# Moving the norm guard, the layer-norm shift and the cell marks from VectorE to GpSimd in an audio tower kernel

## The chip, the cores and the metric

The kernel runs on one core of a Trainium2 chip. The metric is device time in microseconds (us) for one execution of the whole program. Engines are named as the profile names them: PE (TensorE), DVE (VectorE), ACT (ScalarE), POOL (GpSimd), SP (SyncE).

## What is computed

The reference takes `x` of 16 x 375 x 64 and works in three stages.

1. A convolution of nine taps to 128 features, scaled by the norm of its window, through tanh, a bias and ReLU. This gives `h0`, 16 batches of 367 positions.
2. A layer norm of `h0`, attention with one head and three windows that share their scores, an output projection, a residual and a second layer norm; added to `h0`.
3. A third layer norm `hn`, then a product-key feed-forward layer. Cut to what matters here:

```
q  = layernorm(hn @ Wq.T + bq) * ln_g + ln_b        # 8 heads of 64
q0, q1 = halves of 32;   s0, s1 = l2norm(q0) @ l2norm(keys0).T, the same for 1
sc0, ix0 = top_k(s0, 16);  sc1, ix1 = top_k(s1, 16)
fs, pos  = top_k(all sums sc0 + sc1, 16);  fi = the sums of the indices there
w = softmax(fs);   out = sum over heads of (gelu(hn . down[fi]) * w) @ up[fi]
```

`l2norm(x)` is `x / max(norm, 1e-12)`; that maximum is the guard of the norms.

## The kernel before, in words

A batch has 367 positions and is worked in three overlapping tiles of 124 (t = 0, 1, 2). `lnr` and `lnm` (reciprocal deviation and shift) exist for three layer norms i = 0, 1, 2: of `h0`, of `res` (after attention) and of `h` (before the feed-forward layer).

Each engine runs one `body(c)` per batch: a list of steps written out by hand, in which steps of different batches and tiles are interleaved (`c + 1` is the next batch). The first and last bodies are unrolled, the middle ones run in a loop of two. Nothing reorders the work: an engine goes through its list, and a step waits on semaphores for what it needs. POOL issues no DMA. SP loads `x` and stores `o_sb`.

What the change and the prediction touch, by engine:

- **Norm guard and scale.** ACT squares the query and leaves the sums `nss` (`q_norms`, L793). POOL's `q_std` forms `qvar`, `std` (a power, L541) and `qguard` (L542). DVE's `q_guard` (L1303) takes `nmx = max(nss, qguard)`, 16 columns. POOL's `q_scale` (L549) raises it to the power -0.5.
- **Layer norms.** DVE's `p1_stats` (L1249, `bns`) and `p1_moments` (L1259, `bna`) make mean and variance; POOL's `p1_rstd` adds epsilon (L509, `lnv`) and takes the power (L510, `lnr`); DVE's `p1_shift` (L1266) makes `lnm = -mean * lnr`; ACT's `p1_ln` (L706) applies both.
- **Choosing cells.** POOL's `rank_sums` scales the ranked values (L569) and forms 50 candidate sums per head, `cs`, in two halves, and the sums of indices `ce` (L575 to L581). DVE's `choose` (L1391, L1393) runs four steps: the 8 best, their removal into `cr`, the next 8, their removal. DVE's `mark` (L1401) writes `taken`: 4096 where `cr` holds the fill value, else 0, 124 x 400. DVE's `sum_exps` and `invert_sums` (L1412, `wrec`) form the softmax denominator. POOL's `select` multiplies `taken` with `ce` (L591) and with the exponentials (L593), `normalise` finishes the weights (L600, L603) with a copy by ACT between (L823).
- **After that.** PE turns and merges the weights (L1088, L1099), ACT writes the digits `eh` (L841), DVE compares them (`one_high`, L1339, `oh`; `one_low`, L1346 and L1349) and forms `wl` (`low_weights`, L1358), PE multiplies `oh` and `wl` (`scatter`, L1114), DVE forms `prod` (L1367), PE the output, DVE `o_sb`.
- **Attention, around it.** PE's `p1_ax` (L1023), `p1_wo` (L1030), DVE's `p1_res` (L1294), PE's scores (L1000), DVE's `p1_smax` (L1279), POOL's `sbias` (L516), ACT's `probs` (L729), DVE's `rden` (L1287).
- **Head of the next batch.** POOL's `p1_norm` (L491, L492, `wnorm`), DVE's `p1_tscale` (L1235), POOL's `p1_h0` (L499, L501, `h0`), then `p1_stats` for i = 0.

POOL's list between two of these points matters below:

```
rank_sums(c,1,0)  p1_rstd(c+1,2)  rank_sums(c,1,1)  p1_norm(c+2)  q_scale(c,2)
p1_h0(c+2)  q_std(c+1,0)  p1_rstd(c+2,0)  rank_sums(c,1,2)  select(c,1)  normalise(c,1)
rank_sums(c,2,0)  rank_sums(c,2,1)  q_scale(c+1,0)
```

(the last line is the top of the next body, in the same names). DVE's list from `choose(0,3)` goes on with `low_weights(2)`, `mark(0)`, `sum_exps(0)`, `q_guard(1)`, `invert_sums(0)`, ranking, `product(2)`, ranking, `p1_res`.

Of the kernel before, what the change touches and what calls it, by code (L numbers as in the profile page):

```python
# [66 lines left out]
def build(nc, x, tok_kernel, tok_bias, wq, bq, wk, bk, wo, bo, gamma, beta, fwq, fbq, lng, lnb,  # L67
# [5 lines left out]
    with ctx:  # L73
        def sb(name, shape, dt=f32):
            return ctx.enter_context(nc.sbuf_tensor(name, shape, dt))

        def sem(name):
            return ctx.enter_context(nc.semaphore(name))
# [348 lines left out]
        def _(pool):  # L427
# [75 lines left out]
            def p1_rstd(c, i):  # L503
                b = c.b
                link = linker(pool, ln_rstd[i], 2, b)
                pool.wait_ge(ln_stats[i], 2 * (b + 1))
                wait(pool, ln_shift[i], b)
                wait(pool, (xl_ready, xh_ready, hn_ready)[i], b)
                link(g.tensor_tensor(lnv[i][:, :], bna[i][:, :, 1], eps3[:, :], ALU.add))  # L509
                link(g.tensor_tensor(lnr[i][:, :], lnv[i][:, :], power[0:NT, 0, 0:3], ALU.pow), wait=False)  # L510

# [21 lines left out]
            def q_std(c, t):  # L533

                n = c.tile(t)
                link = linker(pool, std_ready, 3, n)
                pool.wait_ge(qss_ready, n + 1)
                wait(pool, std_turned, n)
                wait(pool, nmx_ready, n)
                link(g.tensor_tensor(qvar[:, :], qss[:, :], eps8[:, :], ALU.add))  # L540
                link(g.tensor_tensor(std9[:, 0:H], qvar[:, :], power[0:NT, 1, 0:H], ALU.pow), wait=False)  # L541
                link(g.tensor_tensor(qguard[:, :], qvar[:, :], guard8[:, :], ALU.mult), wait=False)  # L542

            def q_scale(c, t):

                n = c.tile(t)
                pool.wait_ge(nmx_ready, n + 1)
                wait(pool, vals_scaled, 2 * (n - 1))
                g.tensor_tensor(qscale[c.slot(t)][:, :, :].rearrange("p h s -> p (h s)"), nmx[:, :, :].rearrange("p h s -> p (h s)"),  # L549
                                power[0:NT, 0, :], ALU.pow).then_inc(qscale_ready, 1)  # L550

            def rank_sums(c, t, part):
# [5 lines left out]
                if part == 0:  # L558
                    pool.wait_ge(ranked, 16 * n + 6)
                    wait(pool, chosen, 11 * n - 7)  # L560
# [24 lines left out]
            def select(c, t):  # L585

                n = c.tile(t)
                pool.wait_ge(cells_ready, 3 * (n + 1))
                pool.wait_ge(chosen, 11 * n + 9)
                wait(pool, cells_turned, n)  # L590
                g.tensor_tensor(wcell[:, 2, :, :], taken[:, :, :], ce[:, :, :], ALU.mult).then_inc(weights, 1)  # L591
                pool.wait_ge(exp_ready, n + 1)
                g.tensor_tensor(wsel[:, :, :], taken[:, :, :], cx[:, :, :], ALU.mult).then_inc(weights, 1)  # L593

            def normalise(c, t):

                n = c.tile(t)
                pool.wait_ge(weights, 4 * n + 2)
                pool.wait_ge(chosen, 11 * (n + 1))
# [45 lines left out]
        def _(act):  # L645
# [534 lines left out]
        def _(dve):  # L1180
# [81 lines left out]
            def p1_shift(c, i):  # L1262
                b = c.b
                dve.wait_ge(ln_rstd[i], 2 * (b + 1))
                wait(dve, (xl_ready, xh_ready, hn_ready)[i], b)
                v.scalar_tensor_tensor(out=lnm[i][:, :], in0=bna[i][:, :, 0], scalar=-1.0, in1=lnr[i][:, :],  # L1266
                                       op0=ALU.mult, op1=ALU.mult).then_inc(ln_shift[i], 1)

# [20 lines left out]
            def p1_res(c):  # L1289
# [5 lines left out]
                                xb[:, :, :].rearrange("p t d -> p (t d)"), ALU.add).then_inc(res_ready, 1)  # L1295

            def q_guard(c, t):

                n = c.tile(t)
                dve.wait_ge(nss_ready, n + 1)  # L1300
                dve.wait_ge(std_ready, 3 * (n + 1))
                wait(dve, qscale_ready, n)
                v.tensor_tensor(nmx[:, :, :], nss[:, :, :], qguard[:, :].unsqueeze(2).to_broadcast([NT, H, 2]), ALU.max).then_inc(nmx_ready, 1)  # L1303

# [90 lines left out]

            def mark(c, t):

                n = c.tile(t)
                wait(dve, weights, 4 * n)
                dve.wait_ge(chosen, 11 * n + 8)  # L1400
                v.tensor_scalar(taken[:, :, :], cr[:, :, :], NEG / 2, WSCALE, ALU.is_lt, ALU.mult).then_inc(chosen, 1)  # L1401

            def sum_exps(c, t):
# [4 lines left out]
            def invert_sums(c, t):  # L1408
                n = c.tile(t)
                wait(dve, weights, 4 * n)  # L1410
                dve.wait_ge(chosen, 11 * n + 10)
                v.reciprocal(wrec[:, :], wsum[:, :]).then_inc(chosen, 1)  # L1412


            def body(c):
                do(choose, c + -1, 0, 3)
                do(low_weights, c + -2, 2)
                do(mark, c + -1, 0)
                do(sum_exps, c + -1, 0)
                do(q_guard, c + -1, 1)  # L1420
                do(invert_sums, c + -1, 0)
# [30 lines left out]
                do(p1_moments, c + 1, 0)  # L1452
                do(mark, c + -1, 1)
# [3 lines left out]
                do(p1_shift, c + 1, 0)  # L1457
                do(rank, c + -1, 2, 0, 1)
# [66 lines left out]
```

## Time and profile before

| | |
|---|---|
| time, median of 3 runs | 1542.49 us (1540.91 to 1542.98) |
| the profiled execution: time, span | 1543.36 us, 1541.5 us |
| granted TensorE clock over the span | 0.719 |
| busy: PE, DVE, ACT, POOL | 1254.0, 1324.0, 899.9, 962.9 us |
| HBM traffic | 5 GB/s over the span |

A busy share is an average over the whole span. What a step is worth is read from the chain of waits: at each point the engine that ends the wait counts, whether or not it is the busiest. In a timeline row the number in brackets is the time for which the engine sat idle before the row, and what ended it. Rows of one engine that follow each other overlap a little.

### The profile page before, as it was taken

The numbers are of one execution on the slowest core, as the hardware profiler recorded it, in microseconds if no ns is written. First come the engines' busy times: TensorE is split into PE (matmuls) and PEld (weight loads), VectorE is DVE, ScalarE is ACT, GpSimd is POOL, SyncE is SP. The second block draws the span as 40 slices with busy tenths as digits, with TensorE's granted clock in tenths as the row PEclk, the third lists the DMA queues.
The fourth block names the chain that finished last, engine by engine and source line by source line (L and its number), as shares of the span: only waits on it lengthen the run. The fifth ranks groups of instructions, "written<-read, shape, count | busy, mean of one in ns | idle before, by whom it ended". The sixth has DMA issues, their size and how long they took to land.

```text
span 1541.5 us, 41273 instructions
## 1 busy us (share of the span) xinstructions
PE 1254.0 (81%) x9637; PEld 731.0 (47%) x9637; DVE 1324.0 (86%) x10216; ACT 899.9 (58%) x4107; POOL 962.9 (62%) x1870
## 2 busy tenths in 40 slices
PE   2558989798888888898888878898888889888873
PEld 1324445454546454554645554464545455463343
DVE  3116999999999989898899999899798999999895
ACT  1345675766575674656567476656656666655532
POOL 4233867576766857576575757577485767656452
PEclk9667687787767777685777688576676868675555
DMA  1000000000000000000000000000000000000000
GB/s 38 13 1 6 2 5 8 4 10 4 10 4 3 9 5 9 4 10 3 5 10 4 9 5 10 4 8 6 4 9 4 5 4 6 3 4 4 4 3 7
DMA packets 21499, 10.17 MB, mean 7 GB/s; under 512 B 13495, under 2 KB 21099, under 8 KB 21228
## 3 DMA queue, kind: packets, MB, share of 16 engines
q1 hardware_dynamic: 21228, 7.27, 1.9%
q8 instruction: 83, 1.36, 0.4%
q14 instruction: 188, 1.54, 0.3%
HBM read 4.25 MB, written 3.01 MB: 5 GB/s over the span
## 4 chain that ended last, share of the span: by engine, by line
DVE 47%; PE 21%; POOL 10%; ACT 10%; issue 10%; SPq 1%; DVEq 1%; ACTq 0%; POOLq 0%; DMA 0%
DVE idx L1326 14%; DVE val L1324 8%; DVE scores L1329 7%; PE bankM L1114 4%; DVE cr L1393 3%; DVE oh L1339 3%; PE bankQ L1054 3%; POOL cs L575 2%; DVE best L1391 2%; PE bankS L1078 2%; POOL std L541 2%; PE bankS L1077 2%; ACT act_g L770 1%; ACT sq_junk L779 1%; DVE wl L1358 1%
## 5 line engine op out<-in xcount | busy, mean ns | idle before, releaser
L1326 DVE FIND_INDEX8 idx<-val,scores 124x8 uint16<-124x64 f32 x1536 | 304.3, 216 | 0.0
L1324 DVE MAX8 val<-scores 124x8 f32<-124x64 f32 x1536 | 210.8, 207 | 15.8 <-ACT scores L800 15.1
L1114 PE MATMUL bankM<-wl,oh 128*128 128x16 f16 x5952 | 163.0, 172 | 46.2 <-DVE wl L1358 46.2
L1114 PEld LDWEIGHTS bankM<-wl,oh 128*128 128x128 f16 x5952 | 160.0, 101 | 63.2 <-issue 39.9
L793 ACT ACTIVATE ns_junk<-bankQ 124x32 f32<-124x32 f32 x768 | 139.2, 278 | 36.0 <-PE bankQ L1067 36.0
L1339 DVE TENSOR_SCALAR oh<-eh 128x992 f16<-128x992 int16 x384 | 136.4, 424 | 25.3 <-ACT eh L841 25.3
L1329 DVE MATCH_REPLACE8 scores<-val,scores 124x64 f32<-124x64 f32 x768 | 151.3, 206 | 0.0
L549 POOL TENSOR_TENSOR qscale<-nmx,power 124x16 f32<-124x16 f32 x48 | 139.6, 2908 | 10.2 <-DVE nmx L1303 10.1
L793 ACT ACTIVATION_READ_ACCUMULATOR ns_junk<-bankQ 124x1 f32 x768 | 139.5, 291 | 0.0
L1077 PE MATMUL bankS<-wgk,hnT 128*124 128x512 f32 x192 | 121.0, 716 | 0.0
L1078 PE MATMUL bankS<-bias9k,std9T 9*124 9x512 f32 x192 | 120.8, 711 | 0.0
L1011 PE MATMUL banks<-diag,probs 124*124 124x124 f32 x672 | 107.6, 326 | 12.7 <-ACT diag L738 12.5
L575 POOL TENSOR_TENSOR cs<-val_s 124x64 f32<-124x64 f32 (+4 forms) x480 | 109.2, 261 | 7.5
L591 POOL TENSOR_TENSOR wcell<-taken,ce 124x400 f16<-124x400 f32 x48 | 56.8, 1184 | 87.4 <-DVE taken L1401 46.1
L1011 PEld LDWEIGHTS banks<-diag,probs 124*124 124x124 f32 x672 | 100.1, 236 | 19.7 <-ACT diag L738 18.7
L1326 DVE MATCH_VALUE_LOAD idx<-val,scores 124x8 f32 x1536 | 108.3, 70 | 0.0
L1122 PE MATMUL bankM<-up_x,prod 128*124 128x128 f32 x384 | 91.6, 418 | 18.9 <-DVE prod L1367 18.9
L516 POOL TENSOR_TENSOR sbias<-smax,minus_scale 124x3 f32<-124x3 f32 x48 | 14.4, 301 | 148.1 <-DVE smax L1279 148.1
L779 ACT ACTIVATE sq_junk<-bankQ 124x64 f32<-124x64 f32 x384 | 79.3, 234 | 43.6 <-PE bankQ L1055 43.5
L823 ACT ACTIVATE wcell<-wn 124x400 f16<-124x400 f32 x48 | 27.6, 576 | 127.6 <-POOL wn L600 127.6
L1045 PE MATMUL bankQ<-hnT,down_x 128*128 128x372 f32 x128 | 80.8, 725 | 20.5 <-ACT ns_junk L793 11.2
L1122 PEld LDWEIGHTS bankM<-up_x,prod 128*124 128x124 f32 x384 | 83.8, 319 | 25.4 <-DVE prod L1367 23.8
(195 smaller groups left out, 3302.6 us busy)
## 6 DMA issues: line engine op xcount, KB each, us to landing
x_in<-in_x SPq DMA_DIRECT2D x16, 93.8 KB
x_in<-in_x SPq DMA_DIRECT2D x16, 62.5 KB
out<-o_sb SPq DMA_DIRECT2D x16, 62.0 KB
out<-o_sb SPq DMA_DIRECT2D x16, 61.0 KB
out<-o_sb SPq DMA_DIRECT2D x16, 60.5 KB
x_in<-in_x SPq DMA_DIRECT2D x16, 31.0 KB
fwq_in<-in_L_ffn_Wq SPq DMA_DIRECT2D x1, 256.0 KB
conv_w<-in_L_tok_kernel SPq DMA_DIRECT2D x2, 128.0 KB
```

The source lines that it names most:

```text
L549: g.tensor_tensor(qscale[c.slot(t)][:, :, :].rearrange("p h s -> p (h s)"), nmx[:, :, :].rearrange("p h s -> p (h s)"), power[0:NT, 0, :], ...
L575: g.tensor_tensor(dst[:, :, at:at + m], src[:, :, 0, a:a + 1].to_broadcast([NT, k, m]), src[:, :, 1, 0:m], ALU.add)
L793: last = a.activation(ns_junk[:, i, :], bankQ[0:NT, i * HALF:(i + 1) * HALF], ACT.Square, accum_out=nss[:, i // 2, i % 2:i % 2 + 1])
L1011: last = e.matmul(bankB[0:NT, k * NT:(k + 1) * NT], probs[t][w][:, OFF[k]:OFF[k] + NT], diag[:, w, :], start=w == windows[0], stop=w == wi ...
L1077: e.matmul(part, hnT[c.par][:, t, :], wgk[:, 2 * k:2 * k + 2, :].rearrange("p k n -> p (k n)"), start=True, stop=False)
L1078: last = e.matmul(part, std9T[:, :], bias9k[:, 2 * k:2 * k + 2, :].rearrange("p k n -> p (k n)"), start=False, stop=True)
L1114: last = e.matmul(coef[:, g, :, :], oh[:, k, g, :, :].rearrange("p v t -> p (v t)"), wl[:, part, k, :, TG * g:TG * (g + 1)], start=k + par ...
L1122: last = e.matmul(ffn, prod[:, l, :], up_x[:, l, :], start=l == 0, stop=l == EL - 1)
L1324: last = v.max(out=v_[:, hd, s, best8], in_=src[:, hd, s, :])
L1326: last = v.max_index(out=i_[:, hd, s, best8], in_max=v_[:, hd, s, best8], in_values=src[:, hd, s, :])
L1329: last = v.match_replace(out=src[:, hd, s, :], in_to_replace=v_[:, hd, s, best8], in_values=src[:, hd, s, :], imm_value=NEG)
L1339: last = v.tensor_scalar(by_shift[:, :, :, value, :], eh[:, :, :, :].rearrange("p s k (g t) -> p s (k g) t", t=TG), float(value), None, AL ...
```

## The change

Three steps leave DVE's list. `q_guard` becomes three operations in POOL's `q_scale`: subtract `qguard`, maximum with 0, add `qguard` (then the power, as before). `p1_shift` becomes a multiplication of the mean by -1 and a product at the end, in POOL's `p1_rstd`. `mark` becomes the first operation of POOL's `select`. The order of all other steps stays, on all engines. The semaphore `chosen` counts ten per tile instead of eleven, and a new semaphore `marked` lets DVE's `choose` of the next tile overwrite `cr` only once it was read.

```diff
 def p1_rstd(c, i):                                  # POOL
-    link = linker(pool, ln_rstd[i], 2, b)
+    link = linker(pool, ln_rstd[i], 3, b)
     pool.wait_ge(ln_stats[i], 2 * (b + 1))
-    wait(pool, ln_shift[i], b)
     wait(pool, (xl_ready, xh_ready, hn_ready)[i], b)
-    link(g.tensor_tensor(lnv, bna[.., 1], eps3, ALU.add))
-    link(g.tensor_tensor(lnr, lnv, power, ALU.pow), wait=False)
+    link(g.tensor_tensor(lnv, bna[.., 1], eps3, ALU.add), wait=False)
+    link(g.tensor_scalar(lnn, bna[.., 0], -1.0, None, ALU.mult))
+    link(g.tensor_tensor(lnr, lnv, power, ALU.pow))
+    g.tensor_tensor(lnm, lnn, lnr, ALU.mult).then_inc(ln_shift[i], 1)
 def q_std(c, t):                                    # POOL
-    wait(pool, nmx_ready, n)
 def q_scale(c, t):                                  # POOL
-    pool.wait_ge(nmx_ready, n + 1)
+    pool.wait_ge(nss_ready, n + 1)
+    spread = qguard[:, :].unsqueeze(2).to_broadcast([NT, H, 2])
+    pool.wait_ge(std_ready, 3 * (n + 1))
+    g.tensor_tensor(nmx, nss, spread, ALU.subtract).then_inc(nmx_ready, 1)
+    pool.wait_ge(nmx_ready, 3 * n + 1)
+    settled(pool, passed_pool)
+    g.tensor_scalar(nmx, nmx, 0.0, None, ALU.max).then_inc(nmx_ready, 1)
+    pool.wait_ge(nmx_ready, 3 * n + 2)
+    g.tensor_tensor(nmx, nmx, spread, ALU.add).then_inc(nmx_ready, 1)
+    pool.wait_ge(nmx_ready, 3 * n + 3)
 def select(c, t):                                   # POOL
-    pool.wait_ge(chosen, 11 * n + 9)
+    pool.wait_ge(chosen, 10 * n + 8)
+    settled(pool, passed_pool)
+    g.tensor_scalar(taken, cr, NEG / 2, WSCALE, ALU.is_lt, ALU.mult).then_inc(marked, 1)
+    pool.wait_ge(marked, n + 1)
 def p1_moments(c, i):                               # DVE
-    wait(dve, ln_rstd[i], 2 * b)
+    wait(dve, ln_shift[i], b)
 def choose(c, t, step):                             # DVE
+    if step == 1 and q == 0:
+        wait(dve, marked, n)
-def p1_shift(c, i): ...                             # DVE, 3 a batch
-def q_guard(c, t): ...                              # DVE, 3 a batch
-def mark(c, t): ...                                 # DVE, 3 a batch
```

`settled` is a semaphore increment on the engine's own queue. ACT's `q_norms` waits for the same overwritten `nss` as before, now by `nmx_ready` at `3 * n - 2`, the subtraction.

## Rows read from the trace of the kernel before

**Rows 1.** The page: busy time of each engine, and the chain that ended last.
```profile
PE 1254.0 (81%) x9637; PEld 731.0 (47%) x9637; DVE 1324.0 (86%) x10216; ACT 899.9 (58%) x4107; POOL 962.9 (62%) x1870
...
DVE 47%; PE 21%; POOL 10%; ACT 10%; issue 10%; SPq 1%; DVEq 1%; ACTq 0%; POOLq 0%; DMA 0%
```

**Rows 2.** One batch, from one `res` to the next: busy time in that window.
```profile
328.40:413.90 85.50, 73.72 (x602) 43.97 (x602) 81.09 (x638) 55.50 (x258) 60.11 (x114) 0.76 0.03 6
```

**Rows 3.** Groups by line and shape, DVE: the three steps that leave. Busy, mean ns, idle before.
```profile
L1303 DVE TENSOR_TENSOR nmx<-nss,qguard 124x16 f32<-124x16 f32 x48 | 17.3, 360 | 6.4 <-ACT ns_junk L793 6.4
L1401 DVE TENSOR_SCALAR taken<-cr 124x400 f32<-124x400 f32 x48 | 16.9, 352 | 0.0
...
L1266 DVE SCALAR_TENSOR_TENSOR lnm<-bna,lnr 124x3 f32<-124x3 f32 x48 | 13.4, 280 | 12.5 <-POOL lnr L510 11.1
```

**Rows 4.** Timeline of POOL around that batch: start us, us, operation, idle before.
```profile
324.88 0.94 POOL L603 TENSOR_TENSOR wcell<-wn,wcell 124x400 f16<-124x400 f32 x1 [0.65 <-ACT wcell L823]
...
336.96 1.03 POOL L575 TENSOR_TENSOR cs<-val_s 124x64 f32<-124x64 f32 x5
...
339.78 0.27 POOL L509 TENSOR_TENSOR lnv<-bna,eps 124x3 f32<-124x3 f32 x1 [1.40 <-DVE bna L1259]
340.13 0.92 POOL L510 TENSOR_TENSOR lnr<-lnv,power 124x3 f32<-124x3 f32 x1
...
341.50 1.69 POOL L575 TENSOR_TENSOR cs<-val_s 124x64 f32<-124x64 f32 x5
...
348.75 1.17 POOL L501 TENSOR_SCALAR h<-h 124x384 f32<-124x384 f32 x1 [0.20 <-POOL h L499]
...
355.17 1.02 POOL L591 TENSOR_TENSOR wcell<-taken,ce 124x400 f16<-124x400 f32 x1
...
360.67 0.94 POOL L603 TENSOR_TENSOR wcell<-wn,wcell 124x400 f16<-124x400 f32 x1 [2.55 <-ACT wcell L823]
...
364.61 0.40 POOL L569 TENSOR_TENSOR val_s<-val,qscale 124x128 f32<-124x128 f32 x1 [1.14 <-DVE val L1324]
```

**Rows 5.** Timeline of DVE in the same batch.
```profile
345.08 1.26 DVE L1358 TENSOR_TENSOR wl<-wm,ol 128x992 f16<-128x992 f16 x2
...
350.03 0.67 DVE L1249 BATCH_NORM_STATS2 bns<-h 124x6 f32<-124x128 f32 x3
...
353.35 0.37 DVE L1266 SCALAR_TENSOR_TENSOR lnm<-bna,lnr 124x3 f32<-124x3 f32 x1 [0.29 <-POOL lnr L510]
...
366.18 0.17 DVE L1303 TENSOR_TENSOR nmx<-nss,qguard 124x16 f32<-124x16 f32 x1
366.26 0.99 DVE L1391 MAX8 best<-cs 124x8 f32<-124x50 f32 x8
...
377.76 0.36 DVE L1401 TENSOR_SCALAR taken<-cr 124x400 f32<-124x400 f32 x1
```

**Rows 6.** The chain of waits in the same batch: start us, us, what.
```profile
344.69 2.90 POOL qscale L549
...
405.47 0.67 DVE wl L1358
...
406.37 3.36 PE bankM L1114 x124
...
413.85 0.57 DVE res L1294
```

**Rows 7.** Groups by line and shape, POOL: the nearest prices for the new operations.
```profile
L575 POOL TENSOR_TENSOR cs<-val_s 124x16 f32<-124x16 f32 x96 | 23.9, 249 | 0.0
...
L501 POOL TENSOR_SCALAR h<-h 124x384 f32<-124x384 f32 x16 | 18.8, 1172 | 3.2 <-POOL h L499 3.2
...
L440 POOL TENSOR_SCALAR key_n<-key_n 64x2 f32<-64x2 f32 x1 | 0.2, 212 | 14.1 <-DVE key_n L1187 14.1
```

**Rows 8.** Timeline of two engines in another batch.
```profile
761.80 1.04 POOL L591 TENSOR_TENSOR wcell<-taken,ce 124x400 f16<-124x400 f32 x1 [8.53 <-DVE taken L1401]
761.83 1.04 DVE L1303 TENSOR_TENSOR nmx<-nss,qguard 124x16 f32<-124x16 f32 x1
```

More of the change, by code:

```diff
@@ L152, in build @@
         lnm = [sb(f"lnm{i}", [NT, 3]) for i in range(3)]
+        lnn = [sb(f"lnn{i}", [NT, 3]) for i in range(3)]
         xl = sb("xl", [NT, 3, D])
@@ L286, in build @@
         chosen = sem("chosen")
+        marked = sem("marked")
         weights = sem("weights")
@@ L504, in p1_rstd @@
                 b = c.b
-                link = linker(pool, ln_rstd[i], 2, b)
+                link = linker(pool, ln_rstd[i], 3, b)
                 pool.wait_ge(ln_stats[i], 2 * (b + 1))
-                wait(pool, ln_shift[i], b)
                 wait(pool, (xl_ready, xh_ready, hn_ready)[i], b)
-                link(g.tensor_tensor(lnv[i][:, :], bna[i][:, :, 1], eps3[:, :], ALU.add))
-                link(g.tensor_tensor(lnr[i][:, :], lnv[i][:, :], power[0:NT, 0, 0:3], ALU.pow), wait=False)
+                link(g.tensor_tensor(lnv[i][:, :], bna[i][:, :, 1], eps3[:, :], ALU.add), wait=False)
+                link(g.tensor_scalar(lnn[i][:, :], bna[i][:, :, 0], -1.0, None, ALU.mult))
+                link(g.tensor_tensor(lnr[i][:, :], lnv[i][:, :], power[0:NT, 0, 0:3], ALU.pow))
+                g.tensor_tensor(lnm[i][:, :], lnn[i][:, :], lnr[i][:, :], ALU.mult).then_inc(ln_shift[i], 1)
             def p1_sbias(c, t):
@@ L546, in q_scale @@
                 n = c.tile(t)
-                pool.wait_ge(nmx_ready, n + 1)
+                pool.wait_ge(nss_ready, n + 1)
+                spread = qguard[:, :].unsqueeze(2).to_broadcast([NT, H, 2])
+                pool.wait_ge(std_ready, 3 * (n + 1))
+                g.tensor_tensor(nmx[:, :, :], nss[:, :, :], spread, ALU.subtract).then_inc(nmx_ready, 1)
+                pool.wait_ge(nmx_ready, 3 * n + 1)
+                settled(pool, passed_pool)
+                g.tensor_scalar(nmx[:, :, :], nmx[:, :, :], 0.0, None, ALU.max).then_inc(nmx_ready, 1)
+                pool.wait_ge(nmx_ready, 3 * n + 2)
+                g.tensor_tensor(nmx[:, :, :], nmx[:, :, :], spread, ALU.add).then_inc(nmx_ready, 1)
+                pool.wait_ge(nmx_ready, 3 * n + 3)
                 wait(pool, vals_scaled, 2 * (n - 1))
@@ L559, in rank_sums @@
                     pool.wait_ge(ranked, 16 * n + 6)
-                    wait(pool, chosen, 11 * n - 7)
+                    wait(pool, chosen, 10 * n - 6)
                     wait(pool, exp_ready, n)
@@ L588, in select @@
                 pool.wait_ge(cells_ready, 3 * (n + 1))
-                pool.wait_ge(chosen, 11 * n + 9)
+                pool.wait_ge(chosen, 10 * n + 8)
+                settled(pool, passed_pool)
+                g.tensor_scalar(taken[:, :, :], cr[:, :, :], NEG / 2, WSCALE, ALU.is_lt, ALU.mult).then_inc(marked, 1)
+                pool.wait_ge(marked, n + 1)
                 wait(pool, cells_turned, n)
@@ L598, in normalise @@
                 pool.wait_ge(weights, 4 * n + 2)
-                pool.wait_ge(chosen, 11 * (n + 1))
+                pool.wait_ge(chosen, 10 * (n + 1))
                 g.tensor_tensor(wn[:, :, :], wsel[:, :, :], wrec[:, :].unsqueeze(2).to_broadcast([NT, H, NC]), ALU.mult).then_inc(weights, 1)
@@ L790, in q_norms @@
                 act.wait_ge(q2_done, n + 1)
-                wait(act, nmx_ready, n)
+                wait(act, nmx_ready, 3 * n - 2)
                 for i in range(2 * H):
@@ L816, in best_exps @@
                 n = c.tile(t)
-                act.wait_ge(chosen, 11 * n + 6)
+                act.wait_ge(chosen, 10 * n + 6)
                 a.activation(best_exp[:, :, :], best[:, :, :], ACT.Exp).then_inc(best_exp_ready, 1)
@@ L1260, in p1_moments @@
                 last.then_inc(ln_stats[i], 1)
[L1262 to L1267, printed above, removed]
             def p1_smax(c, t):
@@ L1295, in p1_res @@
                                 xb[:, :, :].rearrange("p t d -> p (t d)"), ALU.add).then_inc(res_ready, 1)
[L1297 to L1303, printed above, removed]
             def rank(c, t, half, step):
@@ L1380, in choose @@
                 n = c.tile(t)
-                base = 11 * n + 2 * step
+                base = 10 * n + 2 * step
                 for q in range(2):
@@ L1394, in choose @@
                     last.then_inc(chosen, 1)
[L1396 to L1401, printed above, removed]
             def sum_exps(c, t):
@@ L1410, in invert_sums @@
                 wait(dve, weights, 4 * n)
-                dve.wait_ge(chosen, 11 * n + 10)
+                dve.wait_ge(chosen, 10 * n + 9)
                 v.reciprocal(wrec[:, :], wsum[:, :]).then_inc(chosen, 1)
@@ L1417, in body @@
                 do(low_weights, c + -2, 2)
-                do(mark, c + -1, 0)
                 do(sum_exps, c + -1, 0)
-                do(q_guard, c + -1, 1)
                 do(invert_sums, c + -1, 0)
@@ L1439, in body @@
                 do(one_high, c + -1, 0, 0)
-                do(p1_shift, c, 2)
                 do(one_high, c + -1, 0, 1)
                 do(one_low, c + -1, 0)
-                do(q_guard, c + -1, 2)
                 do(choose, c + -1, 1, 0)
@@ L1452, in body @@
                 do(p1_moments, c + 1, 0)
-                do(mark, c + -1, 1)
                 do(sum_exps, c + -1, 1)
@@ L1465, in body @@
                 do(finish, c + -1, 0)
-                do(q_guard, c, 0)
                 do(choose, c + -1, 2, 0)
@@ L1475, in body @@
                 do(one_low, c + -1, 1)
-                do(mark, c + -1, 2)
                 do(p1_smax, c + 1, 1)
```

2 lines of the change are left out of this document (removed).

## Prediction, made before the changed kernel was built or run

> **What bounds the kernel now.** The page comes first [rows 1]. DVE is busy 86% of the span and PE 81%, so DVE looks like the bound and 144 instructions taken from it look like pure gain. The chain that ended last warns against that: only 47% of it is DVE, 21% PE, 10% POOL. A step is worth what it costs on the chain at its own place.
>
> Second, one batch [rows 2]. From one `res` to the next 85.5 us pass; the five busy times are PE 73.7, weight loads 44.0, DVE 81.1, ACT 55.5, POOL 60.1. DVE idles 4.4 us a batch; POOL has 25 us free, but not everywhere.
>
> Third, POOL's timeline and the chain of waits in that batch [rows 4, 6]. From the `lnv` at 339.78 to the end of `h0` at 349.92 POOL never stops, apart from short waits on its own results. The long power at 344.69 is itself a piece of the chain [rows 6]. DVE's `bns` on `h0` starts at 350.03 [rows 5], 0.11 us after `h0` is done. So this stretch of ten microseconds is bound by POOL already, and four of the new operations go into it.
>
> Fourth, the chain before `res` [rows 6]: DVE's last `wl` ends at 406.14, PE scatters for 3.36 us, then works through three more products, and `res` starts at 413.85. That distance of 7.7 us is PE's. A DVE step taken out behind `wl` only makes DVE wait longer at `res`.
>
> **What leaves DVE.** By the groups [rows 3] it is 17.3 + 16.9 + 13.4 = 47.6 us busy and up to 18.9 us idle ahead of it: 66.5 us for 48 tiles, the most that DVE can shed. By place, a batch has nine of these steps, and a slot is what the next instruction moves up by:
> - `mark(0)` and `q_guard(1)` stand between `wl` and `res`. Elsewhere that guard takes 1.04 us instead of 0.17, beside POOL's `wcell` that began just before it [rows 8, 5]. All of it is worth nothing, since PE sets `res`.
> - The shifts i = 1, 2 and `q_guard(2)` stand between `res` and the `bns` at 350.03. The shift i = 1, some 0.1 us, lets POOL's `lnv` start that much earlier; the others end in a wait for POOL.
> - Behind the `bns`: the shift i = 0, 0.29 idle and 0.37 busy, 0.66; `q_guard(0)` 0.08 (366.18 to 366.26) [rows 5]; `mark(1)` and `mark(2)`, 0.36 each less the overlap of 0.09 that neighbours have, 0.27 each. Sum 1.28 us a batch. This part counts.
>
> **What POOL gets, priced by its own rows.** A small product is 0.25 us (16 columns), a small operation with a constant 0.21 [rows 7]; a wait on its own result costs 0.08 (lnv ends 340.05, the power starts 340.13), with the extra semaphore increment 0.20 (the bracket at 348.75) [rows 4].
> - Shift: constant 0.21, wait 0.08, product 0.20, less overlap: 0.45.
> - Guard: 0.25 + 0.20 + 0.21 + 0.08 + 0.25 + 0.08, about 1.0 with the overlap at the start.
> - Mark: 400 columns by one operation with a constant. The nearest row has 384 columns and takes 1.17 [rows 7], so 1.22; but it has one arithmetic step and the mark two. Bounds: 1.0, the price of a plain product of that size (1.02 at 355.17, [rows 4]), and 2.4, every step at full price. I take 1.25, plus 0.1 for the increment and the wait.
> - In all 3 x (0.45 + 1.0 + 1.35) = 8.4 us a batch: POOL goes from 60 to 68.5 of 85, not a bound as an average.
>
> **The stretch up to `h0`.** Between 339.78 and 349.92 lie one shift (i = 2) and one guard (tile 2): +1.45. Off it go the 0.11 of slack, the 0.1 by which `lnv` starts earlier, and perhaps 0.3: the `cs` group takes 1.69 us against 1.03 undisturbed [rows 4] because it runs beside DVE's `oh`; it will start 0.45 later and `oh` end 0.36 sooner, so about half of that 0.66 goes. The `bns` on `h0` thus comes 0.95 us later than now, counted from `res`. The next-late thing is DVE's `bns`, with all ranking of tile 2 behind it. At `tscale`, just ahead, DVE waits for POOL's `wnorm` too, but has 4.9 us of work from there to the `bns`, and that wait is hidden in this one.
>
> **The stretch behind it.** POOL arrives 0.95 later, adds the shift i = 0 (0.45) and mark(1) (1.35): 2.75 late at `wn`. It idled 2.55 us before `wcell` (360.67) for ACT; where nothing is late ACT's copy takes 0.65 of that (324.88) [rows 4], so 1.9 are absorbed and 0.85 left. The last `val_s` waited 1.14 for DVE (364.61), which absorbs the rest. `choose` of tile 2 is then set by DVE: 0.95 - 0.27 - 0.66 - 0.08 = -0.06, and mark(2) makes it -0.33 at the next `wl` and so at the next `res`.
>
> **Waits that are new.** `q_scale` now waits on POOL for ACT's `nss`; the DVE guard that waited for it stood earlier and had no idle time ahead of it in this batch [rows 5], so POOL doesn't stop, though all its list queues behind. `choose` waits for the mark of the tile before, which ends some 9 us ahead (mark(1) by about 358, while `choose` of tile 2 begins at 366.26): nothing. mark(2) sits behind `sbias`, where POOL idles. Mark(0) and guard(1) fill POOL's idle time before `lnv` i = 1, where `res` sets the start. ACT's and PE's lists are unchanged, and SP's.
>
> **Sum.** 15 batch intervals x (-0.3) = -4.5 us. At both ends of the span, where engines wait for each other tile by tile, the guard and the mark are slower on POOL in series (1.0 for 0.17 plus a hand-over, 1.35 for 0.36): for the first and the last tile +1.7 each at most, taken as +2.5. Total -2.0. The profiled execution took 1543.36 us (span 1541.5 and 1.9 around it), 0.9 above the median of the runs. So 1542.5 - 2.0 = 1540.5.
>
> **Rivals.**
> 1. *DVE stays the bound throughout.* POOL's new operations cost less in their place (shorter, or hidden because `cs` no longer collides with `oh`), and the `bns` on `h0` comes no later. Then a batch saves 1.28: 15 x 1.28 = 19, less 2.5: 1526. The floor is all of rows 3, 66.5 us: 1476, which needs `res` to follow DVE. For it: DVE is 95% busy in the batch. Against it: the 0.11 us at 350.03. Chance 0.27.
> 2. *Slower: POOL late at tile 2's cells.* Place: the last `cs` before `choose(2,0)`. It decides when the added time before it passes 0.95 + 1.9 + 1.14, that is when a mark costs over 1.5 us or the guard over 1.4. With the mark at 2.4 DVE waits about 0.9 more: 15 x (0.9 - 0.3) + 2.5 = +11.5: 1554. Chance 0.18. The unpriced second arithmetic step speaks for it.
> 3. *Slower: the mark holds up `wl`.* A DVE and a POOL operation shut each other out at times [rows 8]. mark(0) is released as the two `wl` begin; if it gets in between them, the second waits 1.2 us, and `res` with it, through PE. 15 x (1.2 - 0.3) + 2.5 = +16: 1558. Against it: at 345.08 both `wl` took 1.26 beside POOL's power of 2.90 [rows 5, 6], as much as two cost anywhere. Chance 0.1.
>    [...]
> 4. *Nearly nothing changes*, the balance worked out above, its parts between -0.5 and +0.2 a batch: 1537 to 1548. Chance 0.45.
>
> **Numbers.** About 0.2%, 3.1 us, is what a measurement of this kernel can tell from no change. Case 4 holds 0.31 of no change, 0.09 of faster and 0.05 of slower. So faster is 0.27 + 0.09 = 0.36, the same 0.31, slower 0.18 + 0.1 + 0.05 = 0.33. The likeliest case gives 1540.5; the range reaches to case 1 and case 2: 1523 to 1557.
>
> **What the profile of after would show.** Right: DVE busy near 1285; POOL busy near 1095; idle time before DVE's `bns` on `h0` of about 1 us a batch, ended by POOL's L501 line, and more idle time before `res` than now; TENSOR_SCALAR `taken` on POOL at 1.2 to 1.3 us. Wrong: no idle time before that `bns` (case 1), waits for `cs` before `best` (case 2), or `wl` pairs over 2 us (case 3). The whole falls if `res` turns out not to be PE's: batches would then get shorter by the slots of mark(0) and guard(1) too.

## The result, and the profile after

The changed kernel took 1554.78 us (median of 6 runs, 1549.07 to 1557.77) against 1541.57 for the one before: ratio 1.0086, 95% interval 1.0065 to 1.0107. It is slower by 0.86%; forecast were 1540.5 and no change. 1554.78 lies inside the range of 1523 to 1557, near its end, but the likeliest case, the balance of case 4, did not come. The profiled execution of after took 1557.77 us, span 1555.7, granted clock 0.716 (before 0.719).

The page of after, busy times and the chain that ended last, against [rows 1]:

```profile
PE 1258.3 (81%) x9637; PEld 732.8 (47%) x9637; DVE 1292.1 (83%) x10072; ACT 897.7 (58%) x4107; POOL 1120.8 (72%) x2158
...
DVE 40%; POOL 22%; PE 17%; issue 10%; ACT 8%; SPq 1%; POOLq 1%; DVEq 0%; DMA 0%; ACTq 0%
```

DVE lost 31.9 us of work and POOL got 157.9. DVE's share of the chain fell from 47 to 40%, POOL's rose from 10 to 22%: the work went from one part of the chain into another, at five times its price (157.9 against 31.9).

What DVE waited for, before and then after (total us, times, longest):

```profile
DVE res L1294 <- PE banks L1030: 18.0, 14, 8.9
...
DVE lnm L1266 <- POOL lnr L510: 11.1, 18, 3.2
...
DVE bns L1249 <- POOL h L501: 8.4, 2, 5.0
...
DVE best L1391 <- POOL cs L581: 4.2, 4, 1.4
```

```profile
DVE bns L1263 <- POOL h L503: 30.9, 16, 4.8
DVE res L1301 <- PE banks L1044: 28.2, 15, 10.9
...
DVE best L1392 <- POOL cs L592: 21.8, 31, 1.3
...
DVE wden L1249 <- POOL wnorm L494: 10.2, 16, 2.8
```

The wait for `h0` comes in every batch now, 16 times instead of 2. Three more waits for POOL and PE grew with it: `res` by 10.2 us, `wden` from 2.2, `best` from 4.2. Together the four grew by 58 us, more than the 31.9 us that DVE gained. Not all of that is time lost: a wait costs only what no later wait hides.

POOL's timeline in the batch whose `res` starts at 420.93, against [rows 4] (start us, us, operation, idle before):

```profile
420.07 0.22 POOL L552 TENSOR_TENSOR nmx<-nss,qguard 124x16 f32<-124x16 f32 x1
420.48 0.26 POOL L555 TENSOR_SCALAR nmx<-nmx 124x16 f32<-124x16 f32 x1 [0.19 <-POOL nmx L552]
420.82 0.22 POOL L557 TENSOR_TENSOR nmx<-nmx,qguard 124x16 f32<-124x16 f32 x1
421.12 2.93 POOL L560 TENSOR_TENSOR qscale<-nmx,power 124x16 f32<-124x16 f32 x1
424.01 0.20 POOL L510 TENSOR_TENSOR lnv<-bna,eps 124x3 f32<-124x3 f32 x1
424.18 0.26 POOL L511 TENSOR_SCALAR lnn<-bna 124x3 f32<-124x3 f32 x1
424.52 0.88 POOL L512 TENSOR_TENSOR lnr<-lnv,power 124x3 f32<-124x3 f32 x1
...
433.04 0.36 POOL L510 TENSOR_TENSOR lnv<-bna,eps 124x3 f32<-124x3 f32 x1
433.38 0.67 POOL L511 TENSOR_SCALAR lnn<-bna 124x3 f32<-124x3 f32 x1
434.12 1.03 POOL L512 TENSOR_TENSOR lnr<-lnv,power 124x3 f32<-124x3 f32 x1
...
435.38 0.40 POOL L580 TENSOR_TENSOR val_s<-val,qscale 124x128 f32<-124x128 f32 x1
435.86 1.04 POOL L586 TENSOR_TENSOR cs<-val_s 124x64 f32<-124x64 f32 x5
...
438.35 0.22 POOL L552 TENSOR_TENSOR nmx<-nss,qguard 124x16 f32<-124x16 f32 x1
438.77 0.26 POOL L555 TENSOR_SCALAR nmx<-nmx 124x16 f32<-124x16 f32 x1 [0.20 <-POOL nmx L552]
439.11 0.65 POOL L557 TENSOR_TENSOR nmx<-nmx,qguard 124x16 f32<-124x16 f32 x1
439.84 3.24 POOL L560 TENSOR_TENSOR qscale<-nmx,power 124x16 f32<-124x16 f32 x1
...
444.24 1.17 POOL L503 TENSOR_SCALAR h<-h 124x384 f32<-124x384 f32 x1 [0.20 <-POOL h L501]
...
451.53 1.57 POOL L602 TENSOR_SCALAR taken<-cr 124x400 f32<-124x400 f32 x1 [0.22 <-POOL ce L592]
```

DVE in the same stretch:

```profile
432.19 2.79 DVE L1338 TENSOR_SCALAR oh<-eh 128x992 f16<-128x992 int16 x8
...
437.44 0.55 DVE L1392 MAX8 best<-cs 124x8 f32<-124x50 f32 x4 [0.98 <-POOL cs L592]
...
439.01 1.28 DVE L1357 TENSOR_TENSOR wl<-wm,ol 128x992 f16<-128x992 f16 x2
...
445.44 0.68 DVE L1263 BATCH_NORM_STATS2 bns<-h 124x6 f32<-124x128 f32 x3 [1.38 <-POOL h L503]
...
461.58 0.55 DVE L1392 MAX8 best<-cs 124x8 f32<-124x50 f32 x4 [0.42 <-POOL cs L592]
```

The same steps stand here twice. The guard at 420.07 runs alone and takes 1.05 us up to the power. The one of tile 2 begins at 438.35, `wl` starts at 439.01, and now the addition takes 0.65 instead of 0.22 and the power 3.24 instead of 2.93: 1.49 up to the power and 1.8 with what the power lost. `wl` took 1.28 against 1.26 before the change [rows 5]; here POOL alone paid. Undisturbed, as at 424.01, POOL needs 1.62 us from `lnv` to its next operation where it needed 1.09 (medians), so the shift costs 0.53. At 433.04, beside `oh`, `lnv`, `lnn` and `lnr` are all longer: from `lnv` to the next `val_s` 2.34 us pass, and 2.57 in the median of the batches, where it was 1.30. In exchange `cs` at 435.86 is back at 1.04 from 1.69 [rows 4]. (This batch shows the steps well but is a late one: POOL came to the `lnv` at 433.04 some 0.7 us later than in most batches.) Over eleven middle batches the median start of `bns` on `h0` moved from 21.81 to 24.05 us behind `res`: 2.24 later, where the prediction had 0.95. Of it 0.47 are there already when POOL starts `wnorm`, from the shift; the guard of tile 2 adds the rest.

The groups by line and shape of after show the same in their means, 1974 ns where the row at 451.53 has 1.57 us and 380 where that at 424.18 has 0.26 (busy, mean ns, idle before):

```profile
L602 POOL TENSOR_SCALAR taken<-cr 124x400 f32<-124x400 f32 x48 | 94.7, 1974 | 52.1 <-DVE cr L1394 41.2 <-issue 5.5 <-POOL ce L592 4.0
...
L511 POOL TENSOR_SCALAR lnn<-bna 124x3 f32<-124x3 f32 x48 | 18.2, 380 | 0.1
```

**Which engine pays where the two meet.** In after, POOL's `lnn` ends at 434.04, 0.04 us after one of the eight `oh` ends, and its addition at 439.76, 0.07 us after the first `wl` ends. But DVE pays as well. From the trace of the kernel before:

```profile
1514.60 2.08 DVE L1358 TENSOR_TENSOR wl<-wm,ol 128x992 f16<-128x992 f16 x2
1514.82 1.33 POOL L591 TENSOR_TENSOR wcell<-taken,ce 124x400 f16<-124x400 f32 x1 [6.36 <-issue]
```

The second of these `wl` took 1.50 instead of 0.67 and ended after POOL's product had; the guard of 1.04 us in [rows 8] is the same. So either engine can hold up the other, and the pair in after is one in which POOL did the waiting.

### The profile page after: what moved, and what is told of

It is laid out like the page before. It is cut to its first block, busy times and chain, and to the rows that moved or that the text cites. A ratio compares the mean times of both kernels' runs of the same rounds, so it can differ in the third digit from the quotient of the medians.

```text
span 1555.7 us, 41431 instructions
## 1 busy us (share of the span) xinstructions
PE 1258.3 (81%) x9637; PEld 732.8 (47%) x9637; DVE 1292.1 (83%) x10072; ACT 897.7 (58%) x4107; POOL 1120.8 (72%) x2158
## 4 chain that ended last, share of the span: by engine, by line
DVE 40%; POOL 22%; PE 17%; issue 10%; ACT 8%; SPq 1%; POOLq 1%; DVEq 0%; DMA 0%; ACTq 0%
DVE idx L1325 11%; DVE val L1323 6%; DVE scores L1328 5%; DVE cr L1394 4%; PE bankM L1128 3%; POOL qscale L560 3%; DVE oh L1338 3%; DVE best L1392 2%; POOL cs L586 2%; POOL lnr L512 2%; PE bankQ L1068 2%; POOL std L543 2%; POOL taken L602 2%; DVE wl L1357 2%; PE bankS L1092 2%
## 5 line engine op out<-in xcount | busy, mean ns | idle before, releaser
L1323 DVE MAX8 val<-scores 124x8 f32<-124x64 f32 x1536 | 211.5, 210 | 15.8 <-ACT scores L814 14.4
L1338 DVE TENSOR_SCALAR oh<-eh 128x992 f16<-128x992 int16 x384 | 132.1, 416 | 19.3 <-ACT eh L855 19.3
L602 POOL TENSOR_SCALAR taken<-cr 124x400 f32<-124x400 f32 x48 | 94.7, 1974 | 52.1 <-DVE cr L1394 41.2
L1092 PE MATMUL bankS<-bias9k,std9T 9*124 9x512 f32 x192 | 126.5, 743 | 0.0
L1091 PE MATMUL bankS<-wgk,hnT 128*124 128x512 f32 x192 | 125.0, 738 | 0.0
L1025 PE MATMUL banks<-diag,probs 124*124 124x124 f32 x672 | 110.7, 332 | 14.8 <-ACT diag L752 14.4
L1325 DVE MATCH_VALUE_LOAD idx<-val,scores 124x8 f32 x1536 | 111.9, 73 | 0.0
L586 POOL TENSOR_TENSOR cs<-val_s 124x64 f32<-124x64 f32 (+4 forms) x480 | 99.3, 241 | 7.5
L855 ACT ACTIVATE eh<-bankM,digit_bias 128x248 int16<-128x248 f32 x192 | 73.8, 469 | 34.1 <-PE bankM L1113 34.1
```

The lines of the kernel that those rows point to most:

```text
L586: g.tensor_tensor(dst[:, :, at:at + m], src[:, :, 0, a:a + 1].to_broadcast([NT, k, m]), src[:, :, 1, 0:m], ALU.add)
L602: g.tensor_scalar(taken[:, :, :], cr[:, :, :], NEG / 2, WSCALE, ALU.is_lt, ALU.mult).then_inc(marked, 1)
L1025: last = e.matmul(bankB[0:NT, k * NT:(k + 1) * NT], probs[t][w][:, OFF[k]:OFF[k] + NT], diag[:, w, :], start=w == windows[0], stop=w == wi ...
L1092: last = e.matmul(part, std9T[:, :], bias9k[:, 2 * k:2 * k + 2, :].rearrange("p k n -> p (k n)"), start=False, stop=True)
L1323: last = v.max(out=v_[:, hd, s, best8], in_=src[:, hd, s, :])
L1325: last = v.max_index(out=i_[:, hd, s, best8], in_max=v_[:, hd, s, best8], in_values=src[:, hd, s, :])
```

## Experiments

All ratios are to the kernel before, run on the same chip in the same series; times of different series are compared by their ratios. The runs of before also differ by their granted TensorE clock: in each of the four series 0.001 more of it goes with 0.33 to 0.45 us less (a fit over 19 to 23 runs). The median clocks of the kernels lie between 0.706 and 0.730, against 0.717 to 0.719 of before, so up to some 5 us of a difference can go with the clock; which of the two follows the other, no run shows. Code that is given in words is not the kernel's text. Theory A says: POOL has no idle time between `lnv` i = 2 and `h0`, so what is added there (the guard of tile 2 above all) makes `h0` and all of DVE's ranking behind it late. The rivals are named in the expectations.

**One part each.** The kernel of after with two of the three steps put back on DVE, at their old places:

```diff
 q_scale(c, t):  guard on POOL      # only_guard
 p1_rstd(c, i):  shift on POOL      # only_shift
 select(c, t):   mark on POOL       # only_mark
-the other two on POOL
+the other two on DVE, as before
```

> Theory A (the stretch of POOL's list up to h0 is the chain, so what is put into it costs its own length): the guard of tile 2 took 1.70 us there in the changed kernel and DVE saves 0.08 us a batch behind it, so about +1.5 us a batch: ratio 1.012 to 1.018, and DVE idle before the statistics of h0 of some 25 to 30 us in all. Theory B (a rival: the loss of the whole change comes from the marks, through the cells of tile 2 and through tile 0): ratio 1.000 to 1.003 here. [...]

> Theory A: the shift i = 2 took 1.3 us more in POOL's stretch in the changed kernel, of which 0.7 came back from the candidate sums behind it that no longer ran beside DVE's oh, so the statistics of h0 come 0.5 us later; DVE saves 0.66 us a batch behind them (shift i = 0). Together -0.1 to -0.2 us a batch: ratio 0.997 to 1.000. [...] If DVE's saving counted in full (three slots, 1.1 us a batch): 0.989.

> Theory A: no mark lies in the stretch up to h0. Mark 0 fills idle time of POOL before the layer norm i = 1, mark 1 is 1.6 us and is absorbed by the 1.9 + 1.1 us that POOL waits behind it, mark 2 lies in idle time. DVE saves 0.54 us a batch in places that count: -0.3 to -0.5 us a batch, ratio 0.995 to 0.998. Theory B: the whole loss is here, ratio 1.007 to 1.009, with waits of DVE's best for the sums cs. [...]

Guards alone: 1566.92 us, ratio 1.0159 (1.0110 to 1.0208), worse than the whole change. Shifts alone: 1536.69, 0.9966 (0.9946 to 0.9987). Marks alone: 1537.79, 0.9981 (0.9960 to 1.0003), which is not clear of no change. The three add up to +1.06% against +0.86% for the change. So the guard is the loss. DVE's waits in the kernel with the guards alone:

```profile
DVE bns L1275 <- POOL h L505: 32.0, 16, 5.0
```

That is the wait of after (30.9) with no mark and no shift on POOL. It was 1.69 us in every middle batch.

**A shorter mark.** All three moved, but the mark without its scaling, so `taken` holds 1 where it held 4096 (this leaves out that multiplication, and the two scalings that undo it elsewhere):

```diff
-g.tensor_scalar(taken, cr, NEG / 2, WSCALE, ALU.is_lt, ALU.mult)
+g.tensor_scalar(taken, cr, NEG / 2, None, ALU.is_lt)
```

> All three parts moved, as in the change, but the mark is one arithmetic step (1 where cr is the fill value) and the factor 4096 is left out of the weights: the indices are then not scaled down, and the output is not scaled back, so the weights are kept in half precision at a smaller size. Theory A: the mark falls from 1.57 us undisturbed towards 1.2; the waits of best for cs (22 us in all) fall by up to 0.4 us a batch; the wait before h0's statistics stays: ratio 1.003 to 1.007. Theory B: it falls to 1.002 or less.

1556.68 us, 1.0108 (1.0061 to 1.0155). The mean of `taken` fell from 1974 to 1635 ns, 16 us of POOL's time, and no gain is seen. The second arithmetic step costs 0.34 us, and its length is not what binds. (The median clock was 0.708 against 0.7135 of after, which could hide some 2 us.) The expected 1.003 to 1.007 was missed by a little.

**Which guard.** The guard of tile 2 alone, and those of tiles 0 and 1 alone:

```diff
 # guard_t2: guard on POOL for t == 2; guard_t01: for t in (0, 1)
-guard(0), guard(1), guard(2); shift(0..2); mark(0..2) on POOL
+only the named guards on POOL, the rest on DVE
```

> Only the guard of tile 2 moves to POOL, the one that lies between wnorm and h0 in POOL's list. Theory A (the place decides): the whole loss of the three guards is in it, ratio 1.013 to 1.018, DVE's wait before the statistics of h0 near 1.7 us a batch. Theory C (all guards cost alike): 1.005.

> Only the guards of tiles 0 and 1 move to POOL. Theory A: both lie where POOL has idle time behind them, and DVE saves 0.08 us a batch that counts: ratio 0.998 to 1.002. Theory C: 1.010.

Tile 2: 1551.74 us, 1.0069 (1.0046 to 1.0092). Tiles 0 and 1: 1538.31, 0.9991 (0.9968 to 1.0015). The wait for `h0` comes whole with the guard of tile 2:

```profile
DVE bns L1275 <- POOL h L505: 32.1, 16, 5.0
```

The place is right, but the size is not: 15 x 1.69 = 25 us were expected and 10 came. This was open until the last series below.

**The change without that guard, and without any.**

```diff
 # no_guard2: as after, but guard(2) on DVE
 # no_guard:  as after, but all guards on DVE
```

> The change with the guard of tile 2 alone left on VectorE; all else is moved. Theory A (the guard of tile 2 makes h0 late by 1.7 us a batch): the idle time of VectorE before bns on h0 falls from 30.9 us to about 10, as where the shift or the mark was moved alone (10.1), and the time falls from 1554.8 to 1540 to 1546, not to the time of before less 8, because mark(0) and guard(1) are still together ahead of lnv i=1 and POOL is late there: idle time at lnm or bns on h0 up to 0.5 us in some batches. Rival (the sum of POOL's new work counts, wherever it stands): a ninth of the guard's share is gone and the time stays above 1550. Rival 2 (the clock of TensorE): no tie to the place of the guard; the time goes with the granted clock alone.

> Marks and shifts moved, all guards on VectorE. Theory A: neither h0 nor lnv i=1 is held up by a guard, so the time is that of the two parts alone, 0.9966 and 0.9981 of before, together 0.993 to 0.997: 1531 to 1537. VectorE busy about 1291, POOL about 1060. Idle time before bns on h0 about 10 to 13 us, because both the shift and the mark lengthen POOL's list. Rival (the parts aren't additive, each of them uses up the same idle time of POOL): 1538 to 1545.

Without the guard of tile 2: 1539.74 us, 1.0003 (0.9990 to 1.0016). Without any: 1530.77, 0.9948 (0.9931 to 0.9965), the product of the two parts alone (0.9966 x 0.9981 = 0.9947). One guard of 1.8 us a batch carries the change's whole loss, 13 us; the other two cost 9 more where marks and shifts are moved too, though alone they cost nothing. DVE's wait for `h0` falls to 11.6 us without the guard of tile 2, while its wait for `cs` stays at 21.3: that second wait stands beside the loss and doesn't make it.

**What stands ahead of `res`.** The prediction costed mark(0) and guard(1) at nothing. This kernel moves these two and nothing else:

```diff
+mark(0) and guard(1) on POOL, the rest on DVE     # before_res
```

> Only the mark of tile 0 and the guard of tile 1 move, the two steps that stand on DVE between wl and res. If PE sets the start of res, DVE's wait before res grows by what leaves DVE there (0.4 to 1.2 us a batch) and the time stays: ratio 0.998 to 1.002. If DVE set it: 0.990 to 0.995. If the mark on POOL got in between the two wl: 1.01.

1556.46 us (1545.84 to 1562.50 in 10 runs), 1.0077 (1.0044 to 1.0111): the expected 0.998 to 1.002 was missed. POOL in the batch whose `res` starts at 771.4, one of the late ones:

```profile
763.42 2.39 POOL L614 TENSOR_SCALAR taken<-cr 124x400 f32<-124x400 f32 x1 [3.33 <-DVE cr L1432]
...
771.63 2.94 POOL L571 TENSOR_TENSOR qscale<-nmx,power 124x16 f32<-124x16 f32 x1
774.52 0.20 POOL L515 TENSOR_TENSOR lnv<-bna,eps 124x3 f32<-124x3 f32 x1
```

`lnv` starts 3.1 us after `res` where DVE's `bna` would let it at 1.8; in the median of eleven batches it is 2.45. The mark beside `wl` takes 2.39 instead of 1.57, then come the guard's 1.05. Of POOL's idle time of 1.6 us there 0.4 are left with the marks alone and 0.5 with guards 0 and 1 alone; with both nothing is. DVE then waits 19.6 us for `lnr` (11.1 before), and `res` 27.5 us for PE (18.0 before): that PE sets `res` was right. In this trace DVE comes to `choose` of tile 2 0.9 us later in the mean of twelve batches, and the fifteen batch intervals are 11.6 us longer in all. The runs of this kernel spread over 17 us, twice as far as those with guards 0 and 1 alone, and the time goes with the clock: two runs at 0.713 and 0.722 took 1546 us, eight at 0.703 to 0.711 took 1550 to 1562. At the slope above, the median clock of 0.707 against 0.7175 goes with some 5 of the 15 us.

**`h0` ahead of the scale.** All three moved, and POOL's `p1_h0` ahead of `q_scale(2)`:

```diff
-do(q_scale, c, 2)
 do(p1_h0, c + 2)
+do(q_scale, c, 2)
```

> The changed kernel, with p1_h0 ahead of q_scale(2) in POOL's list. Theory A in its narrow form (only the start of h0's statistics is late by POOL): the wait there goes and the ratio falls to about 0.995. In its wide form (POOL has no idle time from the moments of i = 1 to the cells of tile 2): POOL now waits about 1.5 us for ACT's tanh, the wait before h0's statistics goes, and comes back larger before best of tile 2; ratio 1.005 to 1.02.

1586.49 us, 1.0305 (1.0268 to 1.0342). DVE's wait for `h0` falls from 30.9 to 10.2 us and two others take its place, of DVE and of POOL:

```profile
DVE best L1430 <- POOL cs L603: 65.7, 43, 4.8
```

```profile
POOL h L503 <- ACT th L716: 40.2, 16, 4.2
```

ACT's `th` was not ready at the earlier place, so POOL idled 2.5 us a batch, and DVE waited 3.1 to 5.8 us in each of nine middle batches for the cells of tile 2. This order mends nothing, and it is worse than both forms of the theory had (0.995, and 1.005 to 1.02). As a test of theory A it is half spoilt, since the idle time is POOL's wait for ACT and not its work.

**Only what stands at a good place.** Mark(2) (behind `sbias`, where POOL idles) and the shift i = 0 on POOL; then mark(1) as well:

```diff
+mark(2), shift(0) on POOL, the rest on DVE              # mark2_shift0
+mark(1), mark(2), shift(0) on POOL, the rest on DVE     # mark12_shift0
```

> Only the two steps that stand behind h0 and where POOL has idle time: mark(2) behind sbias, and the shift of layer norm 0. Theory A: VectorE's saved slots are 0.27 and 0.66 us a batch, nothing is put into POOL's stretch ahead of h0, so 15 x 0.93 = 14 us off, less what is given back at tile 2's cells (the shift makes cs of tile 2 0.5 later, which 1.9 of idle time absorbs): 1528 to 1533, ratio 0.991 to 0.995. Idle time before bns on h0 8 to 10 us as before. Rival (a slot that VectorE gives up becomes a wait for PE at res): ratio 0.997 to 1.0, with the idle time before res up by as much.

> As the kernel with mark(2) and the shift of layer norm 0, and mark(1) on POOL as well, which stands between bns on h0 and the cells of tile 2. Theory A: 0.27 us a batch more off VectorE, but POOL is 1.57 later at select(1); with the shift that is 2.0 us against 1.9 of idle time before wcell and 1.1 before val_s, so it is absorbed: 1524 to 1533, at most 4 us below the kernel with mark(2). If POOL has no idle time there (wide form of theory A), the best waits for cs: its idle time above 10 us against 4, and the time 3 us or more above that kernel.

The first took 1505.26 us, 0.9773 (0.9749 to 0.9796), 34 us less than before. The second took 1526.85, 0.9917 (0.9893 to 0.9941), inside its expected 1524 to 1533 but 22 us above the first, where 4 below was the most expected. The first is far below its expected 1528 to 1533, in part by a mechanism that the expectation didn't have. Its page:

```profile
PE 1234.4 (82%) x9637; PEld 725.6 (48%) x9637; DVE 1307.5 (87%) x10184; ACT 898.9 (60%) x4107; POOL 1000.4 (66%) x1918
```

DVE saved 16.5 us of work; 34 can't come from there.

**Where POOL's loop lies.** POOL's timeline of the kernel before, at the place where its loop jumps back, in an even batch of the loop:

```profile
801.72 0.94 POOL L603 TENSOR_TENSOR wcell<-wn,wcell 124x400 f16<-124x400 f32 x1 [2.41 <-ACT wcell L823]
804.74 0.40 POOL L569 TENSOR_TENSOR val_s<-val,qscale 124x128 f32<-124x128 f32 x1 [2.08 <-DVE scores L1329]
```

The 2.08 us are put down to DVE, but in the next batch, with DVE at the same point, `val_s` follows `wcell` at once, 33.8 us behind `res` instead of 35.6. Such a stop (2.0 to 3.1 us) stands in four even batches of the loop in before, after and every other kernel so far, but not in guard_t2 and mark2_shift0. These two also loaded 168 instruction packets over the run where the others loaded 186 to 189. Counting POOL's queue between two jumps gives 368 entries in before, 372 and 373 in those two, 374 to 432 in the rest. So the size alone doesn't sort them; where the loop starts in the instruction stream could. The test moves the loops with writes to an unused column while POOL idles 14 us at the start:

```diff
 g.memset(key_z, 0.0)
+for k in range(20):          # 60 in before_pad60
+    g.memset(padding[:, k:k + 1], 0.0)
```

Theory L says that the place where the loop starts decides on the stop. By the author's estimate of these places, 20 writes take the stop and 20 packets away in the kernel before (1522 to 1532 us) and bring them back in mark2_shift0 (1518 to 1528) and guard_t2 (1560 to 1568), and 60 writes leave the kernel before as it is (0.998 to 1.003). How much of the stream has to fit for that, no run shows. The rivals are in the expectations.

> The kernel before, with 20 writes of one unused column by GpSimd at its start, where it idles 14 us; nothing else. [...] Rival S (the stop belongs to what the steps do, such as a wait that came late): stop and time stay, ratio 0.998 to 1.002.

> The kernel before with 60 such writes. [...] If any padding helps (by time at the start of the program or otherwise), it is as fast as with 20.

> The kernel with mark(2) and the shift of layer norm 0 on GpSimd, its loop of 373 instructions moved by 20. [...] Rival S: it stays at 1505 (1502 to 1511).

> The kernel with the guard of tile 2 alone on GpSimd, its loop of 372 instructions moved by 20. [...] Rival S: it stays at 1549 to 1554.

The page's queue row, of before and of before with 20 writes, and then that kernel's POOL at the jump, where the stop is gone:

```profile
q14 instruction: 188, 1.54, 0.3%
```

```profile
q14 instruction: 169, 1.38, 0.3%
```

```profile
800.10 0.94 POOL L606 TENSOR_TENSOR wcell<-wn,wcell 124x400 f16<-124x400 f32 x1 [2.40 <-ACT wcell L826]
801.00 0.40 POOL L572 TENSOR_TENSOR val_s<-val,qscale 124x128 f32<-124x128 f32 x1
```

| kernel | stop at the jump | time | ratio |
|---|---|---|---|
| before, 20 writes | gone | 1536.37 | 0.9965 (0.9938 to 0.9991) |
| before, 60 writes | stays | 1543.36 | 1.0013 (0.9997 to 1.0030) |
| mark2_shift0, 20 writes | comes back | 1519.93 | 0.9862 (0.9835 to 0.9888) |
| guard_t2, 20 writes | comes back | 1559.89 | 1.0128 (1.0098 to 1.0158) |

All four went the way theory L said, with stop and packets together, and the work of each pair is the same. The price, by the ratios, was 5 us in the kernel before (10 to 19 were expected), 14 in mark2_shift0 and 9 in guard_t2. DVE's wait for `cs` shows part of it: with the stop it is 4.2, 8.4 and 4.5 us in these three kernels, without it none, 0.5 and none. What the rest is, no view shows. By the count of POOL's entries in the traces, the loops without a stop (368 to 373 long) start at entry 708, 710 and 712; loops of 368 to 374 that start at 692 and from 724 on have it, and so has one of 380 at 713. So the place counts as well as the length; what lies at the edge, no run shows.

With the stop in both kernels, the guard of tile 2 costs 18 us of the 25 of its waits, and mark(2) with the shift i = 0 gains 21 us where slots of 14 were counted. With the stop in neither, it is 0.9773 against 0.9965, some 30 us. A few us of either go with its higher clock (0.726 and 0.7295); the rest of what lies above 14 is not explained. Against that kernel's 0.9862, mark(1) raised the time to 0.9917: some 8 us lost for a slot worth 4, with DVE's wait for `cs` at 11.6 us.

## Why the prediction was wrong, point by point

**The bound.** Right: POOL is the chain from the `lnv` of i = 2 to `h0`, and one guard there is the loss (1.0086 to 1.0003 when it alone goes back). Right too that PE sets `res`: the wait there rose by 10.2 us as DVE's slots ahead of it went.

**The sizes in that stretch: the step that failed.** The prediction put "+1.45" there, "about 1.0" for the guard and 0.45 for the shift, all from rows in which POOL ran undisturbed. Undisturbed they were near (1.05 and 0.53). At their place the guard took 1.8 us beside `wl`, and the shift 1.27 beside `oh` (2.57 - 1.30), of which 0.65 came back from `cs` where 0.3 was allowed. The `bns` on `h0` came 2.24 us later, not 0.95. Put 2.24 into the prediction's own sum and a batch gets 2.24 - 1.28 = 0.96 longer, 15 x 0.96 = 14.4 us; the fifteen intervals between the first and the last `res` got 11.7 us longer (1301.0 to 1312.7). That the two are so near is in part luck, since two more terms offset each other: DVE stood 0.4 us a batch for `cs` of tile 2, and got back 0.9 from there to the next `res` where mark(2) is worth 0.27 (its wait for ACT's `eh` fell from 25.3 to 19.3 us). The forecast used the slowing of `cs` beside `oh` (1.69 for 1.03) as a credit that would go away, which it did, and didn't charge the same to the new operations next to it. In the pairs shown above the operation that took longer ended after the one it ran beside: POOL's `lnn` and its addition 0.04 and 0.07 us after an `oh` and a `wl`, and the `wl` of 1.50 us 0.54 us after POOL's product. The power is different: at 345.08 a pair of `wl` ran through it at 1.26 us [rows 5, 6]. Read against rival 3, the sign is the reverse in these batches: `wl` had started first, kept its 1.28 us, and POOL waited.

**"Mark(0) and guard(1) fill POOL's idle time before `lnv` i = 1"**: failed as a pair. With 2.39 + 1.05 us they used up the 1.6 us of idle time and made `lnv` 0.6 us late in the median, in a kernel of their own worth +0.77%. In after POOL still reaches the `lnv` of i = 2 in time in most batches (11.40 us behind `res`, 11.49 before). With the guard of tile 2 back on DVE it is 0.4 to 0.9 us late there in three of eleven batches, without any guard in none; that fits the 9 us between those two kernels, but no run isolates it.

**The mark**, taken at 1.25: 1.57 undisturbed, of which 0.34 are the second arithmetic step, and 1.97 as a mean. That passes rival 2's threshold of 1.5, and rival 2's time of 1554 is what came; its wait is in the trace too (21.8 us for `cs`, from 4.2). It isn't the cause of the loss: the marks alone gave 0.9981, 0.34 us less in each changed nothing, and with the guard of tile 2 back on DVE that wait stays at 21.3 and the loss is gone. That rival 2 had the right number was luck.

**"1.9 are absorbed"** at `wcell`, and the rest at `val_s`: in part. DVE waits for tile 2's `cs` at 461.58 by 0.42, and in the loop's even batches by 1.2 and again by 1.3, where POOL's stop at the jump has used up that idle time already. The prediction looked at an unrolled batch, in which there is no jump. One more wait wasn't seen: the shift i = 2 stands between the two halves of tile 1's `cs`, so `best` waits 0.98 at 437.44 (0.54 in most batches). It lies ahead of the `bns` and costs nothing of its own.

**Gains behind `h0`** (1.28 a batch): real. With nothing in the full stretch, mark(2) and shift(0) gained 21 us with the stop in both kernels, more than the 14 of their slots.

**Ends of the span**, +2.5: measured +2.6 (first `res` 3.2 later, the tail 0.6 shorter).

**Busy times.** DVE 1292.1 for about 1285 and POOL 1120.8 for about 1095. The largest part of the 26 us on POOL is `taken`: 94.7 us where 48 x 1.25 = 60 were counted, 15 of the difference by its undisturbed price of 1.57 and 19 by the slowing beside DVE. That slowing is no idle time in any row and so is easily missed.

## What to carry to other kernels

Before moving a step to another engine, look at what the first engine runs at the new place: price the step by a row in which both are busy, and count each idle stretch once for all that is put into it. Move only the steps that land where the new engine idles: two of the nine gave 0.9862, all nine 1.0086. And when an edit changes the length or place of a loop, compare instruction packets and the gap at the jump first, for here they were worth 5 to 14 us with no work changed.

The version with mark(2) and shift(0) on GpSimd beats both kernels: 1505.26 us, 0.9773 (0.9749 to 0.9796), of which the loop's lucky place is some 14 us.

## What the hardware showed that was not expected

- POOL's stop of 2.0 to 3.1 us at its loop's jump, with 20 more instruction packets over the run, switched off and on by 20 unrelated writes at the program's start. The profile puts it down to a semaphore of DVE. A loop of 432 entries, that of after, had it too; none above 373 was seen without.
- `taken` of 124 x 400 takes 1.57 us alone and 2.39 beside `wl` on POOL; one arithmetic step is 0.34. DVE did it in 0.352 [rows 3].
- POOL's 3- and 16-column operations, 0.20 to 0.26 us alone, take up to 0.78 beside `wl` or `oh`, and the 16-column power 3.24 instead of 2.93 when a `wl` is running as it starts. The other way round, a `wl` that meets POOL's 400-column product takes 1.50 instead of 0.67, but one that meets the power isn't longer.
